# AdaLN block with a gated recurrence and experts: normalising the input rows on ScalarE instead of VectorE

## What is computed

```python
h = _layernorm(x, axis=-1) * (1 + ca) + sa          # (x - mean) / sqrt(var + eps)
# gated recurrence over h:
u = h @ W_in + b_in
gate_x = sigmoid(u @ W_gx + b_gx); gate_a = sigmoid(u @ W_ga + b_ga)
log_a = -8.0 * gate_a * softplus(a_param); a = exp(log_a)
s_t = a_t * s_(t-1) + sqrt(1 - exp(2 * log_a_t)) * gate_x_t * u_t
x = x + ga * (s @ W_out + b_out)
h = _layernorm(x, axis=-1) * (1 + cb) + sb
x = x + gb * experts(h)      # 8 experts, each takes the 512 rows of a sequence with the highest probability
```

## Time and profile before

| | us |
|---|---|
| median of 3 runs | 1308.64 (1308.49 to 1309.38) |
| the profiled execution | 1307.97 |
| its span | 1305.8 |
| recurrence, from the span's start | 358 |
| selection, until the experts' first lists | 100 |
| experts, to the end | 847 |

### The profile page before, as it was taken

The page is one execution under the profiler, slowest core; times in us unless marked ns, Lnnn a source line. Parts: engine busy times, 40 slices in busy tenths (PEclk is TensorE's granted clock), DMA queues, the critical chain, the costliest instruction groups (busy, mean ns, idle before and its releaser), DMA issues.

```text
span 1305.8 us, 19856 instructions
## 1 busy us (share of the span) xinstructions
PE 1082.6 (83%) x7077; PEld 965.4 (74%) x7077; DVE 916.4 (70%) x2394; ACT 482.1 (37%) x736; POOL 443.9 (34%) x352
## 2 busy tenths in 40 slices
PE   6579898989500059999999999989999999988980
PEld 5468787878500049889899899889899898877970
DVE  3678898998489966576675675756675785678562
ACT  2447677777110023332332333322333333333231
POOL 1011122221120033453443543533543543565243
PEclk8789899999755569999999999989999999998985
DMA  5004444321140033243242332333243334337556
GB/s 166 0 17 162 146 161 162 95 83 65 66 72 0 0 106 74 38 90 70 42 90 66 47 85 66 58 71 70 45 88 66 49 83 115 55 99 224 135 164 195
DMA packets 81517, 113.87 MB, mean 87 GB/s; under 512 B 16784, under 2 KB 67600, under 8 KB 80400
## 3 DMA queue, kind: packets, MB, share of 16 engines
q1 hardware_dynamic: 54528, 77.61, 18.1%
q0 software_dynamic: 24576, 34.10, 15.7%
q10 hardware_dynamic: 2320, 0.93, 0.3%
HBM read 62.01 MB, written 50.59 MB: 86 GB/s over the span
## 4 chain that ended last, share of the span: by engine, by line
PE 58%; DVE 4%; issue 1%; DMA 1%; POOL 1%; ACT 1%; DVEq 0%; SPq 0%; POOLq 0%; ACTq 0%
PE psum L1492 28%; PE psum L1510 27%; DVE hidT L1436 3%; PE psum L1469 2%; PE psum L1477 1%; DVE hidT L1438 1%; POOL ffn_rows L1300 0%; DMA w_raw<-ffn_rows 0%; DMA ffn_rows<-rows_y,idx_cur 0%; POOL w_raw L1194 0%; ACT acc L1340 0%; DMA rows_in<-z_rows,idx_cur 0%; DVE place L1388 0%; POOL rows_in L1288 0%; DVEq L1230 0%
## 5 line engine op out<-in xcount | busy, mean ns | idle before, releaser
L1492 PE MATMUL psum<-w,hidT 128*128 128x256 f32 x3072 | 385.6, 287 | 21.0 <-DVE hidT L1438 17.6
L1492 PEld LDWEIGHTS psum<-w,hidT 128*128 128x128 f32 x3072 | 376.8, 193 | 24.3 <-DVE hidT L1438 20.7
L1510 PE MATMUL psum<-xT,w 128*128 128x512 f32 x1536 | 371.8, 398 | 3.5 <-DVE xT L1419 3.5
L1300 POOL DMA_INDIRECT ffn_rows<-rows_y,idx_cur x128 | 214.4, 1675 | 403.2 <-ACT rows_y L1331 362.6
L1510 PEld LDWEIGHTS psum<-xT,w 128*128 128x128 f32 x1536 | 286.4, 189 | 66.4 <-DVE xT L1419 3.9
L1436 DVE CAST hidT<-hf 128x512 fp32r<-128x512 f32 x256 | 141.3, 552 | 243.2 <-ACT hf L1357 243.2
L1357 ACT ACTIVATE hf<-psum 128x512 f32<-128x512 f32 x256 | 153.2, 599 | 207.2 <-PE psum L1510 205.9
L1438 DVE TENSOR_TENSOR hidT<-hf,hidT 128x512 fp32r<-128x512 f32 x256 | 180.4, 705 | 8.8
L1288 POOL DMA_INDIRECT rows_in<-z_rows,idx_cur x128 | 128.1, 1001 | 136.7 <-DVE idx_cur L1401 98.6
L1331 ACT ACTIVATE rows_y<-psum,g_cur 128x256 f32<-128x256 f32 x128 | 53.8, 471 | 322.0 <-PE psum L1492 235.9
L322 POOL TENSOR_SCALAR ve<-mv 128x4 f32<-128x4 f32 x32 | 21.3, 666 | 286.2 <-DVE mv L454 286.2
(11 more groups left out here) (191 smaller groups left out, 1253.4 us busy)
## 6 DMA issues: line engine op xcount, KB each, us to landing
w_raw<-in_L_ffn_w SPq DMA_DIRECT2D x16, 1024.0 KB, 6.5
x_buf<-in_L_attn_x SPq DMA_DIRECT2D x16, 512.0 KB, 5.5
x_rows<-x SPq DMA_DIRECT2D x16, 512.0 KB, 2.9
z_rows<-z SPq DMA_DIRECT2D x16, 512.0 KB, 3.2
ffn_rows<-zero_row SPq DMA_DIRECT2D x8, 1024.0 KB, 7.3
res_t<-x_rows SPq DMA_DIRECT2D x16, 512.0 KB, 5.6
w_raw<-ffn_rows SPq DMA_DIRECT2D x16, 512.0 KB, 6.2
out_x<-res_t SPq DMA_DIRECT2D x16, 512.0 KB, 5.2
```

Of the source, the lines that this page charges most:

```text
L1300: pool.indirect_dma_start(acc_dram, bass.IndirectOffsetOnAxis(ap=idx_cur[n][:, b, t:t + 1], axis=0), rows_y[u.n % 2][:, t, :], None, compu ...
L1492: ins = pe.matmul(Y_tok[:, t, :], hidT[qs][:, k, t * P:(t + 1) * P], w2_s[n][qm][:, k, :], start=(x_ == 0), stop=(x_ == len(terms) - 1))
L1510: ins = pe.matmul(H_bank[m % 4], w1_s[n][qs][:, k, m * P:(m + 1) * P], xT[qm][:, k, :], start=(x_ == 0), stop=(x_ == len(terms) - 1))
```

## The change

DVE no longer writes z1. Instead it computes, behind the same wait for rstd, a shift of -mean * rstd for each row, one small instruction per group into the new tile nm1 (`shift1`, semaphore r_nm). ACT computes z1 = x * rstd + shift, four ACTIVATEs with the function Identity, whose scale and bias come by pointer from rs1 and nm1. In a step, ACT does this behind the square root (`scale`) and ahead of the `warm` activation; for the first group it does it ahead of the loop. The waits for r_T1 (z1's buffer is free again) go along to ACT. PE, and all other work, is as before.

```diff
--- before.py
+++ after.py
@@ -169,6 +169,7 @@
         mv1 = [sbr(f"mv1_{n}", [P, TT, 2]) for n in range(2)]
         ve1 = sbr("ve1", [P, TT])
         rs1 = [sbr(f"rs1_{n}", [P, TT]) for n in range(2)]
+        nm1 = [sbr(f"nm1_{n}", [P, TT]) for n in range(2)]
         z1 = [sbr(f"z1_{n}", [P, TT, D]) for n in range(2)]
         hT_z = [sbr(f"hT_z{q}", [P, KD, GT], F32R) for q in range(2)]
         ta = sbr("ta", [P, KD, GT])
@@ -227,6 +228,7 @@
         r_st1 = sem("stats1_read")
         r_mv1 = sem("mean_var1_ready")
         r_rs1 = sem("rstd1_steps")
+        r_nm = sem("shift1_ready")
         r_z1 = sem("z1_ready")
         r_T1 = sem("z1T_in_psum")
         r_hi = sem("hT_z_hi_ready")
@@ -353,6 +355,16 @@
                     act.wait_ge(s_wp, n + 1)
                     act.activation(W[0][:], ps[:, :, 0:D], ACT.Copy).then_inc(s_hi, 1)
 
+                def norm1(g):
+
+                    act.wait_ge(r_nm, g + 1)
+                    if g >= 2:
+                        act.wait_ge(r_T1, g - 1)
+                    for t in range(TT):
+                        ins = act.activation(z1[g % 2][:, t, :], x_buf[g % XR][:, t, :], ACT.Identity,
+                                             bias=nm1[g % 2][:, t:t + 1], scale=rs1[g % 2][:, t:t + 1])
+                    ins.then_inc(r_z1, 1)
+
                 def hi_z(g):
 
                     act.wait_ge(r_T1, g + 1)
@@ -417,8 +429,9 @@
                         act.wait_ge(r_p, g)
                     act.activation(sc_t[:], a2_t[g % 2][:], ACT.Sqrt, bias=quarter[:, 0:1], scale=0.25).then_inc(r_sc, 1)
 
+                norm1(0)
                 for s in range(1, LAST + 1):
-                    _, c_, r_, _, e_ = stages(s)
+                    a, c_, r_, _, e_ = stages(s)
                     if c_ is not None:
                         hi_z(c_)
                     if e_ is not None:
@@ -429,6 +442,8 @@
                         gate_a(c_)
                         gate_x(c_)
                         scale(c_)
+                        if a is not None:
+                            norm1(a)
                         if c_ + 1 < NG:
                             act.activation(warm[:], quarter[:], ACT.Tanh)
 
@@ -461,15 +476,13 @@
                         dve.wait_ge(r_z1, g - 1)
                     stats(g, x_buf[g % XR], st1, mv1, r_st1, r_mv1)
 
-                def norm1(g):
+                def shift1(g):
 
                     dve.wait_ge(r_rs1, 2 * g + 2)
                     if g >= 2:
-                        dve.wait_ge(r_T1, g - 1)
-                    for t in range(TT):
-                        ins = dve.tensor_scalar(z1[g % 2][:, t, :], x_buf[g % XR][:, t, :], mv1[g % 2][:, t, 0:1],
-                                                rs1[g % 2][:, t:t + 1], ALU.subtract, ALU.mult)
-                    ins.then_inc(r_z1, 1)
+                        dve.wait_ge(r_z1, g - 1)
+                    dve.scalar_tensor_tensor(out=nm1[g % 2][:], in0=mv1[g % 2][:, :, 0], scalar=-1.0, in1=rs1[g % 2][:],
+                                             op0=ALU.mult, op1=ALU.mult).then_inc(r_nm, 1)
 
                 def lo_z(g):
 
@@ -595,7 +608,7 @@
                     step(dve.tensor_tensor(ap["abs"][:], bcol["a"][:], ap["neg"][:], ALU.max))
                     dve.tensor_scalar(half_bgx[:], bcol["gx"][:], 0.5, None, ALU.mult)
                     dve.tensor_scalar(half_bga[:], bcol["ga"][:], 0.5, None, ALU.mult)
-                    norm1(0)
+                    shift1(0)
                     dve.wait_ge(s_exp, 1)
                     step(dve.tensor_scalar(ap["u"][:], ap["exp"][:], 1.0, None, ALU.add))
                     step(dve.tensor_scalar(ap["um"][:], ap["u"][:], -1.0, None, ALU.add))
@@ -688,7 +701,7 @@
                     if d is not None:
                         norm2(d)
                     if a is not None:
-                        norm1(a)
+                        shift1(a)
                     if s == 1:
                         setup_out()
                     if s == 2:
```

## The result

The changed kernel takes 1328.6 us (median, 1327.6 to 1329.35) against 1308.6 (1303.9 to 1309.4): 1.016 times as long, with a 95% interval of 1.0135 to 1.0185. Its profiled execution has a span of 1326.0 us, 20.2 more than before. The forecast was 1333 us, in a range of 1317 to 1344.

What follows compares the result with a forecast made beforehand. It took the step's turn to close on DVE's queue, and on ACT's after the change; 1.6 + 1.65 + 5.8 + 15.5 = 24.6 us on 1307.97 gave 1332.6, or 1333 on the median's scale, range 1317 to 1344.

Steps and rivals of the forecast that it cites:

- part 1: DVE's queue: four TENSOR_SCALARs, 1.38 us a step, go; shift1 at 0.17 us comes; at most 0.35 us reach gated_u.
- the ring: A recurrence step's cycle from one step's transposes to the next's across PE, ACT and DVE: 16.56 us before, 18.01 forecast.
- part 3: A step's turn: 15.95 us to the root's end + 2.00 + 0.06 = 18.01 against 16.56; PE's wait 2.59 us.
- part 2: ACT's four new ACTIVATEs a step: 0.60 us for one, 0.50 start to start, 2.09 in all; lower bound 1.58.
- part 4: Table load, warm-up, hi_z and lo_z behind norm1: lo_z ends about 4.2 us after the transposes, covered by 0.9 us.
- (a): Start: norm1(0) stands in ACT's queue behind gate-weight copies; first transposes at 19.42, not 17.84: +1.6 us.
- (b): Steps 1 to 3: nothing changes in 1 and 2; step 3's turn sends its transposes from 99.83 to 101.48, +1.65 us.
- (c): Twelve turns from 99.83 to 310.13, all 18.01 us: 216.12 against 210.30, +5.8 us, with no fall of the clock.
- (d): Falls of PE's clock: twelve waits x 1.16 = 13.9 us, plus 1.6 for the wait before step 4: 15.5 us.
- the straight line: Clock cost of PE's 2.59 us wait, interpolated between 1.14 (no cost) and 2.97 (mean cost 1.46): 1.16 us each.
- The rival that the clock holds: All PE waits of 2.59 us pass without a fall of the clock: 10.7 us more, 1319 us; chance 20%.
- the one that every turn starts cold: Clock falls after all thirteen PE waits, 1.60 to 2.69 us each: total 30 to 44, 1339 to 1353 us; chance 11%.

Runs made afterwards that it cites:

- the one with waits of 4.0 us: The changed kernel with norm1 and the `warm` activation (with its table load) exchanged in ACT's queue; 1361.3 us, measured in one execution.

## Why the prediction was right, point by point

- *What bounds the step* (before part 1): right that the step closed on DVE's queue, but incomplete. It names DVE's wait of 0.28 us for rstd and not the one of 0.70 for the clip, which puts ACT's exponentials into the ring; this costs the forecast nothing, as the same stretch of ACT is in the changed kernel's ring.
- *The ring and the new turn* (part 3): right. Forecast 18.01 us, measured 17.93 to 17.97. PE's wait was forecast at 2.59 and is 2.51.
- *ACT's part* (part 2): right. The form was not in the trace, and the estimate from two-pointer rows was 0.60 us alone, 0.50 start to start, 2.09 in all. Of the 64 of them:

```profile
L364 ACT ACTIVATE z<-x_buf,nm,rs x64: 583/585/598, 17.4 to 330.4; 128x256 f32<-128x256 f32 x64
```

  and 2.06 us for four. The lower bound from the one-pointer row (1.58) would have been wrong by half a us a step.
- *DVE's relief* (part 1): right. The shift takes 0.16 us; the time freed became a wait of 0.78 us for the root and one of 2 us for hi_z.
- *The cover behind norm1* (part 4): right. hi_z starts 1.37 to 1.48 us after the transposes (forecast 1.48), lo_z ends 4.06 to 4.18 after them (4.2), Wa starts at 5.11. The row on table loads was the better guide than the Trainium skill (ScalarE: Activation LUTs, What ACT_TABLE_LOAD costs), which adds a drain of about 1.38 us to each load: in the changed kernel too hi_z starts at 275.35, 0.23 us after the load's end at 275.12, with the warm-up in between.
- *The sum*: (a), the start, was forecast at 1.6 us and is 2.98. The missing term is a fall of the clock: PE now waits 1.75 us before the first transposes, which then take 1.97 us for eight, not 1.07. In the profiled execution of the kernel with products in PE's wait, which is the same up to step 3, they took 1.10, and step 3's came 1.9 us later than before, near the forecast. (b) is 1.65, as forecast. (c) is 12 x 17.95 - 210.30 = 5.1, forecast 5.8. (d), the falls, was forecast at 15.5 and is 11.1 us; this is the term that was mis-sized, by 4.4 us. That the forecast in all is too high by the same 4.4 us is chance: the 1.4 us missing in (a) are made up by 0.7 too much in (c) and by 0.7 less behind step 16.
- *Why (d) was too high*: the step that failed is the straight line between a wait that never costs and waits that cost 1.46 on average. It charged 1.16 us to each of twelve waits. Six of the twelve waits of 2.51 us had a fall, at 1.57 to 1.64 us each: 0.81 for one in the mean. The thirteenth wait, of 4.29 us, cost 1.33. Two further runs with the same waits agree: the clock fell behind seven of twelve in the one with stats1 ahead of clip and behind six of twelve in the one with z1(0) on DVE. Between a fall and none there is no middle; what the line got wrong is how often it falls, and its slope rested on four waits. The rival that the clock holds and the one that every turn starts cold were both wrong for this kernel, and the second is nearly true for the one with waits of 4.0 us. (The kernel of which the Trainium skill tells in the section that the prediction names, TensorE: Matmul & The Clock Gate, HAM oscillation, waits longer, about 3 to 5 us.)
- *Not foreseen*: nothing of the difference lies behind step 16, but the time there moves by itself, from 990.9 to 999.1 us in the twelve profiled executions, and one part of it is known (below).

## What to carry to other kernels

An engine with more than half its time free over a span may have none at the place where a step turns; before work is moved to it, read what it must finish first there, and write the turn as a sum along that engine's queue. Reordering the bound queue was worth 15.5 us here, moving work off it cost 20: look for a wait inside the full engine's queue (0.70 us for the clip, 0.28 for rstd) before taking work away. And where TensorE waits 2.5 us or more in a step, price the slower clock behind it, and try products for nobody in the wait.

## What the runs showed of the hardware

- From step 4 to step 16 the clock fell behind none of the waits of 1.54 us and less. Behind 2.44 it fell in one of three cases. Behind 2.5 us it fell in 19 of 36 cases, in stretches every other turn; behind 2.6 in two of three, behind 2.7 to 2.8 in five of six, behind 3.1 to 3.3 in six of seven, behind 4.0 us and more always (16 cases). The wait's length alone does not decide: at the start the clock was low behind waits of 1.75, 1.85 and 2.03 us and full behind one of 2.58. Eight matrix products in the wait were enough to hold it.
- One ACTIVATE of 128x256 from SBUF with scale and bias by pointer takes 0.585 us, the one-pointer form from PSUM 0.472.
- PE makes a pause in the experts' stage, at the same place of the program in eleven of the twelve traces, with nothing that it waits for in the profile; in all twelve DVE has a stop of 3.4 to 4.5 us near that place (3.47 in the kernel before). Here it is in the kernel before, then in the changed one:

```profile
852.71 7.54 PE L1492 MATMUL psum<-w,hidT 128*128 128x256 f32 x40 [3.29 <-issue]
```

```profile
873.98 2.40 PE L1505 MATMUL psum<-w,hidT 128*128 128x256 f32 x10 [4.12 <-issue]
```

  It was 1.7 to 5.5 us long in these traces, and absent in the kernel before with products in its waits. Its cause is open. The kernel before itself ran between 1303.2 and 1310.1 us over 13 executions, a spread of the size of this pause; whether the one explains the other was not shown.
